# Wide cross-attention: value and output weights folded per head, context multiplied by them in dense chunks through DRAM, dense probabilities, one exponential per eight heads

## The chip, the cores and the metric

One Trainium2 chip, one core of it. The metric is the device time of one execution in microseconds (us), the median of several runs. The engines are TensorE (PE, with its weight loads as PEld), VectorE (DVE), ScalarE (ACT), GpSimd (POOL) and SyncE (SP); transfers issued by SyncE and ScalarE run as hardware queues.

## The reference

Two decoder layers over `x` of 64 sequences x 128 tokens x 128 channels. The kernel has six stages: Taylor attention, **wide cross-attention**, GELU experts, causal attention, rotary cross-attention, SwiGLU experts. The change touches the second (with residual and layer norm around it). Cut to what matters, for each sequence (SQ = 128 tokens, SK = 77 context tokens, 16 heads of 64):

```
xn   = layernorm(x) * gamma + beta                       # 128 x 128
q    = xn @ w_q                                          # 128 x 1024, 16 heads
k, v = split(context @ w_kv)                             # 77 x 1024 each, 16 heads
p    = softmax(q_h @ k_h.T * 64 ** -0.5, axis=-1)        # 128 x 77, each head
o    = concat_h(p_h @ v_h) @ w_out + b_out               # 128 x 128
x    = layernorm(x + tanh(gate) * o)
```

Then the router of the next stage takes logits of the new `x`, picks two of eight experts for each token, and the tokens are scattered to DRAM, sorted by expert.

## The kernel before

`softmax_attention(chip, "wide", ...)` works on pairs of sequences, 32 in all. Each engine has its own program, written out by hand; the engines meet in semaphores. A loop step has eight slots `k` (`NU` = 8; a slot is four heads of one of the pair's two sequences). In a step different pairs are at different stages: `f` is the pair whose front is made (layer norm, keys, values), `c` the pair whose scores are made (one step later), `u` the one before that, and `n`, `r`, `q`, `ranked` and `later` are older pairs in layer norm, router and scatter. `lagged(c, u, k, lag)` finds the piece of `lag` slots ago. The order of work within a slot is the order in the code, on each engine, and a waiting instruction holds up all behind it on its engine.

Query and key weights are already folded per head at the start of the stage (`product`, 128 x 128 for each head), so the keys of a head are `product` times the context. What one pair does now:

- TensorE: 16 key products of 154 columns in six groups (`front_pe`, m 0 to 5), four value products of 512 columns (m 6 to 9), the transpose of `xn` (m 10); eight score products of 308 columns (four heads x 77); 32 transposes of probabilities, 128 x 77 each (`TLAG` 3 slots later); 32 context products (`PLAG` 4 slots later), each with 64 columns of weights in half the array; at `Y_AT` 6 `project`, 16 products of 128 x 128 with `wo_scaled`. Each product of fp32 data is two instructions in the trace, a transpose one.
- VectorE: for each slot the negated maximum (`neg_max`), a reciprocal of the four sums; for every second slot the copy of the context products to `oT`; `add_and_measure` at `Z_AT` 7; both layer norms; the router's chains of small instructions (`place_block`).
- ScalarE: copies of keys, values and transposed probabilities out of PSUM, and 32 exponentials of 77 columns, one for each head, with the maximum as bias and the sum as accumulator.
- GpSimd: for each slot `probs` = `exps` x `inv_sum`; parts of the layer norms, the residual, and the indirect scatters.
- SyncE: for pair f the load of `xin` (it waits for `z_done` of pair f-4: `RING` = 4 buffers) and of `ctxT`. After the loads of pairs 7, 15, 23 and 31 it issues a quarter of the fill of the second `sorted_x` with blanks, on the same queue; nothing waits for that fill before a much later stage.

Opening the stage, TensorE makes `product` and VectorE scales the output weights with tanh(gate) (`wo_scaled`).

Of the kernel before, what the change touches and what calls it, by code (L numbers as in the profile page):

```python
# [22 lines left out]
P = 128  # L23
F32 = mybir.dt.float32
# [369 lines left out]
def softmax_attention(chip, kind, n_seq, X, ctxT_dram, w, consts, route=None, fill=None, opening=None, later_loads=()):  # L394
# [13 lines left out]
    FU = {"wide": 11, "causal": 4, "rotary": 2}[kind]  # L408
# [14 lines left out]
    with ExitStack() as ctx:  # L423
# [10 lines left out]
        values = sb("values", [P, 2, 2, H, STRIP])  # L434
        keys = sb("keys", [P, 2, H, 2, NK] if kind == "wide" else [P, 2, KH, NK])
        exps = sb("exps", [P, ES, HU, NK])
        if late:
            sums = sb("sums", [P, 2, NC * P])
            inv_total = sb("inv_total", [P, 2, H])
            o = sb("o", [P, 2, H, 8])  # L440
        else:
            exp_sum = sb("exp_sum", [P, SLOTS, HU])
            inv_sum = sb("inv_sum", [P, SLOTS, HU])
            probs = sb("probs", [P, SLOTS, HU, NK])
        probsT = sb("probsT", [P, 2, HU * P])
        neg_max = sb("neg_max", [P, SLOTS, HU])
        oT = sb("oT", [P, 2, 2, P] if late else [P, 2, 2, NC, P])
# [6 lines left out]
        if kind != "causal":  # L454
            ctxT = sb("ctxT", [P, RING, 2, P])
        if kind == "wide":
            xn = sb("xn", [P, 2, P])
# [4 lines left out]
            product = sb("product", [P, H, P])  # L462
# [47 lines left out]
        f_bank, y_bank = chip.banks[:, 6], chip.banks[:, 7]  # L510
        free_at_first = [f_bank, y_bank] + s_bank + p_bank + o_bank
# [11 lines left out]
        READY = {"wide": 2, "causal": 5, "rotary": 5}[kind]  # L523
        ROOT = 3 + 3 * NEWTON
        PREPARED = {"wide": 3, "causal": 4, "rotary": 10}[kind]
# [40 lines left out]

        @block.sync
        def _(sp):
            def step(f):
                if f is None:  # L570
                    return
# [17 lines left out]
            run_steps(sp, step, n_pairs, 1, 4)  # L589
# [40 lines left out]
        def _(pool):  # L630
# [4 lines left out]
            if kind == "rotary":  # L635
                pool.memset(ctxT[:, :, :, NK:P], 0.0).then_inc(ready, 1)
            if kind != "wide":
# [27 lines left out]
            def step(e, roots, f, c, u, n, r=None, *later):  # L665
                for k in range(NU):
# [1442 lines left out]
```

## Time and profile before

| what | value |
|---|---|
| median of 3 runs | 2991.36 us (2991.24 to 2993.08) |
| span of the profiled execution | 3015.3 us |
| TensorE busy over the span | 2737.1 us, 91% |
| ScalarE, VectorE, GpSimd busy | 2070.9, 1805.1, 1460.1 us |
| mean granted clock of TensorE | 0.965 of full speed |
| the wide stage | from about 229 us to about 1145 us |

The span of the profiled execution is 0.8% longer than the median of the runs; nothing else is known of its own time. "Granted clock" is the share of the full TensorE clock of 2.4 GHz, so 0.50 is 1.2 GHz. In the wide stage the loop of 32 pairs runs to about 1098 us; behind it the last blocks of tokens are routed and scattered.

### The profile page before, as it was taken

The numbers are of one execution on the slowest core, as the hardware profiler recorded it, in microseconds if no ns is written. First come the engines' busy times: TensorE is split into PE (matmuls) and PEld (weight loads), VectorE is DVE, ScalarE is ACT, GpSimd is POOL, SyncE is SP. The second block draws the span as 40 slices with busy tenths as digits, with TensorE's granted clock in tenths as the row PEclk, the third lists the DMA queues.
The fourth block names the chain that finished last, engine by engine and source line by source line (L and its number), as shares of the span: only waits on it lengthen the run. The fifth ranks groups of instructions, "written<-read, shape, count | busy, mean of one in ns | idle before, by whom it ended". The sixth has DMA issues, their size and how long they took to land. (4 is left out here: it accounts for less than half of the span.)

```text
span 3015.3 us, 69304 instructions
## 1 busy us (share of the span) xinstructions
PE 2737.1 (91%) x21504; PEld 1982.6 (66%) x21504; DVE 1805.1 (60%) x5293; ACT 2070.9 (69%) x7235; POOL 1460.1 (48%) x1978
## 2 busy tenths in 40 slices
PE   8999999999999956998799999978999999699987
PEld 6666777777777746998355555546776666458874
DVE  6883344443444444554688888876677776444545
ACT  6766778777787743443699999976888888522224
POOL 3442224444444454555433333325678887724665
PEclk9999999999999987999899999998999999799998
DMA  9910030220400402221310000000000010001225
GB/s 264 338 47 15 19 116 16 80 78 20 129 27 20 135 30 72 73 70 57 115 56 10 9 10 8 10 22 10 13 27 28 29 31 17 29 26 56 80 79 185
DMA packets 179960, 185.08 MB, mean 61 GB/s; under 512 B 32844, under 2 KB 168537, under 8 KB 179216
## 3 DMA queue, kind: packets, MB, share of 16 engines
q1 hardware_dynamic: 162032, 145.14, 16.1%
q0 software_dynamic: 17280, 34.13, 3.4%
q8 instruction: 181, 2.97, 0.4%
q14 instruction: 179, 1.47, 0.2%
q10 hardware_dynamic: 288, 1.38, 0.2%
HBM read 58.34 MB, written 111.48 MB: 56 GB/s over the span
## 5 line engine op out<-in xcount | busy, mean ns | idle before, releaser
L678 POOL TENSOR_TENSOR wide_probs<-wide_exps,wide_inv_sum 128x308 f32<-128x308 f32 x256 | 179.3, 700 | 488.9 <-DVE wide_inv_sum L1409 486.0
L1400 DVE TENSOR_REDUCE wide_neg_max<-banks 128x4 f32<-128x308 f32 x256 | 122.5, 478 | 473.6 <-PE banks L982 448.9
L1116 ACT ACTIVATE causal_exps<-causal_biased,causal_neg_max 128x128 f32<-128x128 f32 x1024 | 325.8, 391 | 31.1 <-DVE causal_neg_max L1400 29.7
L1119 ACT ACTIVATE wide_exps<-banks,wide_neg_max 128x77 f32<-128x77 f32 x1024 | 315.8, 326 | 0.3 <-DVE wide_neg_max L1400 0.2
L658 POOL DMA_INDIRECT sorted_x<-send,place_i x240 | 244.9, 1020 | 96.0 <-issue 40.5
L1116 ACT ACTIVATE rotary_exps<-banks,rotary_neg_max 128x77 f32<-128x77 f32 x1024 | 252.0, 351 | 15.1 <-DVE rotary_neg_max L1400 13.7
L1103 ACT ACTIVATE wide_probsT<-banks 77x512 f32<-77x512 f32 x256 | 152.1, 594 | 153.6 <-PE banks L991 149.5
L1656 ACT ACTIVATE gelu_hidden<-banks,gelu_slot 128x256 f32<-128x256 f32 x284 | 116.7, 471 | 157.3 <-PE banks L1833 153.1
L1587 POOL DMA_INDIRECT results<-swiglu_tile_out,swiglu_dest_i x142 | 147.7, 1040 | 141.2 <-DVE swiglu_tile_out L1738 97.8
L1119 ACT ACTIVATION_READ_ACCUMULATOR wide_exps<-banks,wide_neg_max 128x1 f32 x1024 | 213.9, 209 | 0.0
L1587 POOL DMA_INDIRECT results<-gelu_tile_out,gelu_dest_i x142 | 140.8, 991 | 142.3 <-DVE gelu_tile_out L1743 119.0
L1358 DVE TENSOR_TENSOR causal_biased<-banks,regions 128x512 f32<-128x512 f32 x256 | 164.6, 685 | 72.3 <-PE banks L968 69.9
L1400 DVE TENSOR_REDUCE rotary_neg_max<-banks 128x4 f32<-128x308 f32 x256 | 121.5, 475 | 120.8 <-PE banks L982 116.4
L982 PE MATMUL banks<-wide_keys,wide_xT 128*128 128x308 f32 x512 | 191.8, 455 | 1.9 <-ACT wide_xT L769 1.6
L982 PE MATMUL banks<-rotary_keys,rotary_qT 128*128 128x308 f32 x512 | 189.0, 451 | 3.5 <-ACT rotary_exps L1116 3.4
L616 POOL TENSOR_TENSOR rotary_keys<-rotary_kT,rest 128x308 f32<-128x308 f32 x256 | 177.4, 708 | 20.0 <-ACT rotary_kT L803 16.5
L991 PEld LDWEIGHTS banks<-first,causal_exps 128*128 128x128 f32 x1024 | 108.9, 141 | 116.3 <-ACT causal_exps L1116 61.0
L1103 ACT ACTIVATE rotary_probsT<-banks 77x512 f32<-77x512 f32 x256 | 157.7, 616 | 34.7 <-PE banks L991 34.1
L735 PE MATMUL banks<-wide_ctxT,wide_product 128*128 128x154 f32 x1024 | 169.9, 299 | 3.3 <-ACT wide_product L1038 0.7
L1400 DVE TENSOR_REDUCE causal_neg_max<-causal_biased 128x4 f32<-128x512 f32 x256 | 169.6, 673 | 0.5 <-ACT causal_exps L1116 0.4
L991 PE MATMUL banks<-first,causal_exps 128*128 128x128 f32 x1024 | 166.1, 285 | 3.1 <-ACT causal_exps L1116 3.0
L1014 PE MATMUL banks<-wide_probsT,wide_values 77*64 77x128 f32 x2048 | 168.3, 285 | 0.1
(382 smaller groups left out, 7339.3 us busy)
## 6 DMA issues: line engine op xcount, KB each, us to landing
sorted_x<-blank SPq DMA_DIRECT2D x1, 34848.0 KB, 116.8
sorted_x<-blank SPq DMA_DIRECT2D x4, 8712.0 KB, 30.3
gelu_tile_in<-sorted_x SPq DMA_DIRECT2D x71, 132.0 KB
swiglu_tile_in<-sorted_x SPq DMA_DIRECT2D x71, 132.0 KB
gelu_back<-results SPq DMA_DIRECT2D x16, 512.0 KB, 7.7
swiglu_back<-results SPq DMA_DIRECT2D x16, 512.0 KB, 6.2
X<-in_x SPq DMA_DIRECT2D x8, 512.0 KB, 7.3
regions<-in_g_w SPq DMA_DIRECT2D x2, 2048.0 KB, 20.9
```

The source lines that it names most:

```text
L616: engine.tensor_tensor(keys[:, b, heads], kT[:, pair.c % 2, b, 0:NK].unsqueeze(1).to_broadcast([P, HU, NK]), mask[:, heads].unsqueeze(2).t ...
L658: pool.indirect_dma_start(route["sorted_x"], bass.IndirectOffsetOnAxis(ap=r_place_i[:, b % 2, which, n // 2:n // 2 + 1], axis=0), send[:, ...
L678: pool.tensor_tensor(probs[:, m % SLOTS], exps[:, m % SLOTS], inv_sum[:, m % SLOTS].unsqueeze(2).to_broadcast([P, HU, NK]), ALU.mult).then ...
L735: last = pe.matmul(f_bank[:, n * 2 * NK:(n + 1) * 2 * NK], product[:, first + n], ctxT[:, s4, :, 0:NK], start=True, stop=True)
L982: pe.matmul(s_bank[k % 2][:, 0:HU * NK], q, moving, start=True, stop=True).then_inc(s_ps, 1)
L991: last = pe.transpose(p_bank[n % 2][0:NK, h * P:(h + 1) * P], exps[:, (NU * pair.c + n) % ES, h] if late else probs[:, n % SLOTS, h], ident)
L1014: last = pe.matmul(o_bank[g % 2][row:row + STRIP, col:col + P], values[0:NK, pair.c % 2, b, first_head(j) + h], probsT[0:NK, n % 2, h * P: ...
L1103: act.activation(probsT[0:NK, n % 2], p_bank[n % 2][0:NK], ACT.Copy).then_inc(probsT_done, 1)
L1116: last = act.activation(exps[:, (NU * c.c + k) % ES, h], scores[:, h * NK:(h + 1) * NK], ACT.Exp, bias=neg_max[:, k % SLOTS, h:h + 1])
L1119: last = act.activation(exps[:, k % SLOTS, h], scores[:, h * NK:(h + 1) * NK], ACT.Exp, bias=neg_max[:, k % SLOTS, h:h + 1], accum_out=exp ...
L1400: dve.tensor_reduce(neg_max[:, k % SLOTS], scores.rearrange("p (h n) -> p h n", h=HU), AX.X, ALU.max, negate=True).then_inc(max_done, 1)
L1587: pool.indirect_dma_start(results, bass.IndirectOffsetOnAxis(ap=dest_i[:, t % YR, j:j + 1], axis=0), tile_out[:, t % YR, j], None, bounds_ ...
```

## The change

It computes the same with other intermediate values.

- At the start of the stage the value weights and the output weights of each head are multiplied (`fold`, 128 x 2048: 16 heads of 128 x 128, scaled with tanh(gate)). `wo_scaled` and `project` are gone, and so are `values`, `oT` and `o_done` for this stage.
- The context of all sequences is read as 4928 tokens in a row, in 39 chunks of 128 (the last of 64). A chunk times `fold` is four units of 512 columns (`unit`), 156 in all. Three are made ahead of the loop, then five a step, at the slots `V_AT`. ScalarE copies each from `o_bank[1]` to `staged` (`keep_unit`).
- SyncE stores each chunk (1 MB) to `v_dram` and loads it back for each pair in eight transfers (`load_folded`), so that a row of `folded` is one (context token, head), in chunks of 128 rows, five for eight heads (616 rows). The issues for pair t-2 stand behind the loads for pair t in SyncE's program, and behind the fill where there is one.
- The scores have their maximum subtracted by VectorE, into `exps`; one exponential on ScalarE then covers eight heads (616 columns, in place); VectorE sums it, takes the reciprocal, and GpSimd writes the product in the order (token, head).
- The probabilities are transposed in five chunks of 128 for eight heads (`turn_probs`, `TLAG` 4), and `weighted_sum` (`PLAG` 5) adds all 20 products of a pair's two sequences in `o_bank[0]`, which VectorE adds to the residual (`Z_AT` 5). `weighted_sum` of a pair waits for its eight loads and for the last pair's `z`.
- Each pair's `ctxT` for the keys stays; the chunks of context are loaded once more (`v_context`). The wait of `turn_tokens` for `z_done` is dropped in this stage.

```diff
-    FU = {"wide": 11, "causal": 4, "rotary": 2}[kind]
+    FU = {"wide": 7, "causal": 4, "rotary": 2}[kind]
+    HH, PARTS, CHUNKS, SPARE, VU, V_EARLY, EB = 8, 8, 5, 2, 5, 3, 3
+    TOKENS = n_seq * CONTEXT
+    N_UNITS = 4 * ((TOKENS + P - 1) // P)
...
+            def store_chunk(n):
+                rows = min(P, TOKENS - P * n)
+                sp.wait_ge(v_done, 4 * n + 4)
+                sp.dma_start(route["v_dram"][:, P * n:P * n + rows].rearrange("g t c -> t g c"),
+                             staged[0:rows, n % 2].rearrange("p (g c) -> p g c", g=2)).then_inc(v_stored[n % 2], 16)
+
+            def load_folded(pair):
+                last = (2 * CONTEXT * (pair + 1) - 1) // P
+                for n in range(max(0, last - 1), last + 1):
+                    sp.wait_ge(v_stored[n % 2], 16 * (n // 2 + 1))
+                if pair >= SPARE:
+                    sp.wait_ge(pv_done, PARTS * (pair - SPARE + 1))
+                for b in range(2):
+                    for g in range(2):
+                        t = CONTEXT * (2 * pair + b)
+                        sp.dma_start(folded[:, pair % SPARE, b, g, 0:4],
+                                     route["v_dram"][g, t:t + 64].rearrange("(c k) (h d) -> (k h) c d", c=4, h=HH)).then_inc(folded_loaded[pair % SPARE], 16)
+                        sp.dma_start(folded[0:104, pair % SPARE, b, g, 4],
+                                     route["v_dram"][g, t + 64:t + CONTEXT].rearrange("k (h d) -> (k h) d", h=HH)).then_inc(folded_loaded[pair % SPARE], 16)
+
+            def values_step(pair):
+                if pair == 0:
+                    sp.wait_ge(ready, READY)
+                made = (V_EARLY + VU * pair) // 4
+                for n in range(made if pair else 0, min((V_EARLY + VU * (pair + 1)) // 4, N_UNITS // 4)):
+                    store_chunk(n)
+                load_folded(pair)
+
...
+            def step(f, ahead=None, pair=None):
+                if f is not None:
+                    load(f)
+                if kind == "wide" and pair is not None:
+                    values_step(pair.c)
+
+            def load(f):
+                if kind == "wide":
...
-            run_steps(sp, step, n_pairs, 1, 4)
+            run_steps(sp, step, n_pairs, 3 if kind == "wide" else 1, 4)
...
-                    at = None if late else lagged(c, u, k, MLAG)
+                    at = None if late or k % 2 else lagged(c, u, k, 2)
                     if at is not None:
-                        pair, m = at
-                        pool.wait_ge(inv_done, pair.count(NU, m + 1))
-                        if before(pair, m, SLOTS) is not None:
-                            bc, bk = before(pair, m, SLOTS)
-                            pool.wait_ge(probsT_ps, bc.count(NU, bk + 1))
-                        pool.tensor_tensor(probs[:, m % SLOTS], exps[:, m % SLOTS],
-                                           inv_sum[:, m % SLOTS].unsqueeze(2).to_broadcast([P, HU, NK]), ALU.mult).then_inc(probs_done, 1)
+                        half = 4 * at[0].c + at[1] // 2
+                        pool.wait_ge(inv_done, half + 1)
+                        if half >= SLOTS:
+                            pool.wait_ge(probsT_ps, 2 * (half - SLOTS) + 2)
+                        pool.tensor_tensor(probs[:, half % SLOTS, 0:HH * NK].rearrange("p (k h) -> p h k", h=HH), exps[:, half % EB],
+                                           inv_sum[:, half % SLOTS].unsqueeze(2).to_broadcast([P, HH, NK]), ALU.mult).then_inc(probs_done, 1)
...
+        V_AT = [0, 2, 4, 6, 7]
+        FRONT_AT = {"wide": [(0, 0), (1, 0), (2, 0), (3, 0), (4, 0), (5, 0), (7, 0)],
                     "causal": [(0, 0), (1, 0), (2, 0), (3, 0)], "rotary": [(5, 0), (7, 0)]}[kind]
...
-        TLAG, PLAG, OLAG = (2, 3, 4) if late else (3, 4, 5)
-        Y_AT, Z_AT = 6, 7
+        TLAG, PLAG, OLAG = (2, 3, 4) if late else (4, 5, 6)
+        Z_AT = 5
...
+            def unit(v):
+                rows = chunk_rows(v)
+                if v >= 1:
+                    pe.wait_ge(v_done, v)
+                if v % 4 == 0:
+                    pe.wait_ge(v_context_loaded[v // 4 % 4], 16 * (v // 16 + 1))
+                pe.matmul(v_bank[0:rows], v_context[:, v // 4 % 4, 0:rows], fold[:, (v % 4) * 512:(v % 4 + 1) * 512],
+                          start=True, stop=True).then_inc(v_ps, 1)
...
+                for n in range(H // 2):
+                    last = pe.transpose(p_bank[n // 4][:, (n % 4) * P:(n % 4 + 1) * P], w["wv"][:, n * P:(n + 1) * P], ident)
+                    if n % 4 == 3:
+                        last.then_inc(wvT_ps, 1)
+                pe.wait_ge(wvT_done, 2)
+                for n in range(H // 2):
+                    for odd in range(2):
+                        rows = slice(64 * odd, 64 * odd + 64)
+                        last = pe.matmul((p_bank if odd else o_bank)[n // 4][:, (n % 4) * P:(n % 4 + 1) * P], wvT[rows, n], w["wo"][rows, n],
+                                         start=True, stop=True)
+                    if n % 4 == 3:
+                        last.then_inc(fold_ps, 1)
                 pe.wait_ge(product_done, UB)
+                pe.wait_ge(fold_done, 4)
                 pe.wait_ge(prepared, PREPARED)
+                for v in range(V_EARLY):
+                    unit(v)
...
-            def project(u, r, q):
-
-                pe.wait_ge(o_done, u.count(OG, OG))
-                if u.back(1).real:
-                    pe.wait_ge(z_done, u.back(1).count(1, 1))
-                if r is not None:
-                    pe.wait_ge(logits_done, r.count(1, 1))
-                if block_of(q, 3) is not None:
-                    pe.wait_ge(base_done, block_of(q, 3) + 1)
-                for b in range(2):
-                    for n in range(NC):
-                        last = pe.matmul(y_bank[:, b * P:(b + 1) * P], oT[:, u.c % 2, b, n],
-                                         w["wo_scaled" if kind == "wide" else "wo"][:, n], start=n == 0, stop=n == NC - 1)
-                last.then_inc(y_ps, 1)
+            def turn_probs(pair, m):
+                half, part = 4 * pair.c + m // 2, m % 2
+                if part == 0:
+                    pe.wait_ge(probs_done, half + 1)
+                if half >= 1:
+                    pe.wait_ge(probsT_done, 2 * half + part - 1)
+                for n in range(2 if part else 3):
+                    at = (3 * part + n) * P
+                    last = pe.transpose(p_bank[part][:, n * P:(n + 1) * P], probs[:, half % SLOTS, at:at + P], ident)
+                last.then_inc(probsT_ps, 1)
+
+            def weighted_sum(pair, m):
+                half, part = 4 * pair.c + m // 2, m % 2
+                b, g = m // 4, m // 2 % 2
+                pe.wait_ge(probsT_done, 2 * half + part + 1)
+                if m == 0:
+                    pe.wait_ge(folded_loaded[pair.c % SPARE], 16 * 8 * (pair.c // SPARE + 1))
+                    if pair.c >= 1:
+                        pe.wait_ge(z_done, pair.c)
+                for n in range(3 * part, CHUNKS if part else 3):
+                    last = pe.matmul(o_bank[0][:, b * P:(b + 1) * P], probsT[:, half % 2, n * P:(n + 1) * P], folded[:, pair.c % SPARE, b, g, n],
+                                     start=g == 0 and n == 0, stop=g == 1 and n == CHUNKS - 1)
+                last.then_inc(pv_done, 1)
...
+            def keep_unit(v):
+                rows, n = chunk_rows(v), v // 4
+                act.wait_ge(v_ps, v + 1)
+                if v % 4 == 0 and n >= 2:
+                    act.wait_ge(v_stored[n % 2], 16 * (n // 2))
+                act.activation(staged[0:rows, n % 2, (v % 4) * 512:(v % 4 + 1) * 512], v_bank[0:rows], ACT.Copy).then_inc(v_done, 1)
...
+                        half, part = 4 * at[0].c + at[1] // 2, at[1] % 2
+                        columns = slice(3 * P, CHUNKS * P) if part else slice(0, 3 * P)
+                        act.wait_ge(probsT_ps, 2 * half + part + 1)
+                        if half >= 2:
+                            act.wait_ge(pv_done, 2 * half + part - 3)
+                        act.activation(probsT[:, half % 2, columns], p_bank[part][:, 0:(2 if part else 3) * P], ACT.Copy).then_inc(probsT_done, 1)
...
+                    if c is not None and not late and k % 2 == 1:
+                        half = 4 * c.c + k // 2
+                        act.wait_ge(shifted_done, 2 * half + 2)
+                        act.activation(exps[:, half % EB], exps[:, half % EB], ACT.Exp).then_inc(exps_done, 1)
...
+                for n in range(2):
+                    dve.wait_ge(wvT_ps, n + 1)
+                    dve.tensor_copy(wvT[:, 4 * n:4 * n + 4].rearrange("p n c -> p (n c)"), p_bank[n]).then_inc(wvT_done, 1)
+                dve.wait_ge(prepared_ps, UB)
+                by_parity = fold.rearrange("p (n odd d) -> p n odd d", odd=2, d=P)
+                for n in range(2):
+                    dve.wait_ge(fold_ps, n + 1)
+                    for odd in range(2):
+                        dve.tensor_scalar(by_parity[:, 4 * n:4 * n + 4, odd], (p_bank if odd else o_bank)[n].rearrange("p (n d) -> p n d", d=P),
+                                          w["tanh_gate"], None, ALU.mult).then_inc(fold_done, 1)
...
+                    at = None if late or k % 2 else lagged(c, u, k, 2)
+                    if at is not None:
+                        half = 4 * at[0].c + at[1] // 2
+                        dve.wait_ge(exps_done, half + 1)
+                        dve.tensor_reduce(exp_sum[:, half % SLOTS], exps[:, half % EB], AX.X, ALU.add).then_inc(sum_done, 1)
+                        if half >= SLOTS:
+                            dve.wait_ge(probs_done, half - SLOTS + 1)
+                        dve.wait_ge(sum_done, half + 1)
+                        dve.reciprocal(inv_sum[:, half % SLOTS], exp_sum[:, half % SLOTS]).then_inc(inv_done, 1)
...
+                        if kind == "wide":
+                            half = 4 * c.c + k // 2
+                            if half >= EB:
+                                dve.wait_ge(probs_done, half - EB + 1)
+                            dve.wait_ge(max_done, c.count(NU, k + 1))
+                            dve.tensor_tensor(exps[:, half % EB, HU * (k % 2):HU * (k % 2 + 1)], scores.rearrange("p (h n) -> p h n", h=HU),
+                                              neg_max[:, k % SLOTS].unsqueeze(2).to_broadcast([P, HU, NK]), ALU.add).then_inc(shifted_done, 1)
...
+            "fold": cut(region_b, 0, [P, 16 * P]), "product": cut(region_b, 16 * P, [P, 16, P]),
```

## Rows read from the trace of the kernel before

**Rows 1.** The page's first line, and busy us of each engine in one stretch of 100 us
```profile
span 3015.3 us, 69304 instructions
...
500.00:600.00 100.00, 99.06 (x733) 74.62 (x731) 44.24 (x163) 77.16 (x328) 44.68 (x64) 1.00 0.18 55
```

**Rows 2.** SyncE's timeline: start us, duration us, issue; loads of pairs 4 and 31
```profile
293.18 0.46 SPq L576 DMA_DIRECT2D wide_xin<-X  x1
...
1015.44 0.47 SPq L576 DMA_DIRECT2D wide_xin<-X  x1
```

**Rows 3.** TensorE's timeline in one pair: start us, duration us, group
```profile
607.30 1.08 PE L739 MATMUL banks<-regions,wide_ctxT 128*77 128x512 f32 x2
608.22 3.73 PE L944 MATMUL banks<-regions,wide_oT 128*128 128x128 f32 x32
611.79 0.69 PE L982 MATMUL banks<-wide_keys,wide_xT 128*128 128x308 f32 x2
...
617.60 0.68 PE L982 MATMUL banks<-wide_keys,wide_xT 128*128 128x308 f32 x2
618.13 0.60 PE L991 MATMUL banks<-first,wide_probs 128*77 128x128 f32 x4
618.56 0.95 PE L735 MATMUL banks<-wide_ctxT,wide_product 128*128 128x154 f32 x6
619.44 0.66 PE L1014 MATMUL banks<-wide_probsT,wide_values 77*64 77x128 f32 x8
620.03 0.61 PE L886 MATMUL banks<-rest,wide_tokensT 128*128 128x8 f32 x4
```

**Rows 4.** ScalarE's groups of the whole span: busy us, mean ns, idle before
```profile
L1116 ACT ACTIVATE causal_exps<-causal_biased,causal_neg_max 128x128 f32<-128x128 f32 x1024 | 325.8, 391 | 31.1 <-DVE causal_neg_max L1400 29.7
L1119 ACT ACTIVATE wide_exps<-banks,wide_neg_max 128x77 f32<-128x77 f32 x1024 | 315.8, 326 | 0.3 <-DVE wide_neg_max L1400 0.2
...
L774 ACT ACTIVATE wide_keys<-banks 128x462 f32<-128x462 f32 x160 | 89.1, 557 | 26.3 <-PE banks L735 25.4
```

**Rows 5.** VectorE's groups, of the page and of the stretch 400 to 1000 us
```profile
L1400 DVE TENSOR_REDUCE wide_neg_max<-banks 128x4 f32<-128x308 f32 x256 | 122.5, 478 | 473.6 <-PE banks L982 448.9
...
L1358 DVE TENSOR_TENSOR causal_biased<-banks,regions 128x512 f32<-128x512 f32 x256 | 164.6, 685 | 72.3 <-PE banks L968 69.9
...
L1400 DVE TENSOR_REDUCE causal_neg_max<-causal_biased 128x4 f32<-128x512 f32 x256 | 169.6, 673 | 0.5 <-ACT causal_exps L1116 0.4
...
L1422 DVE COPY wide_oT<-banks 128x512 f32<-128x512 f32 x90 | 59.8, 664 | 0.3 <-issue 0.3
...
L1343 DVE TENSOR_TENSOR wide_z<-banks,wide_residual 128x256 f32<-128x256 f32 x22 | 8.7, 395 | 0.0
```

**Rows 6.** GpSimd's costliest group of the page
```profile
L678 POOL TENSOR_TENSOR wide_probs<-wide_exps,wide_inv_sum 128x308 f32<-128x308 f32 x256 | 179.3, 700 | 488.9 <-DVE wide_inv_sum L1409 486.0
```

**Rows 7.** DMA issues: count, KB each, median us from issue to landing
```profile
sorted_x<-blank SPq DMA_DIRECT2D x4, 8712.0 KB, 30.3
...
causal_xin<-X SPq DMA_DIRECT2D x32, 128.0 KB, 2.0
...
regions<-in_alibi ACTq DMA_DIRECT2D x1, 1024.0 KB, 5.1
...
regions<-in_rest SPq DMA_DIRECT2D x1, 16.0 KB, 17.0
```

**Rows 8.** Stretches: engines as in rows 1, then granted clock, DMA share, GB/s
```profile
10.00:15.00 5.00, 4.75 (x24) 3.58 (x23) 1.14 (x3) 2.02 (x8) 0.79 (x2) 1.00 1.20 290
...
230.00:235.00 5.00, 5.00 (x25) 5.00 (x25) 2.14 (x11) 1.71 (x3) 1.44 (x3) 0.50 0.65 169
...
240.00:241.00 1.00, 1.00 (x10) 1.00 (x9) 0.00 (x0) 0.60 (x2) 0.00 (x0) 1.00 0.00 0
...
380.00:400.00 20.00, 19.81 (x143) 14.07 (x142) 7.52 (x25) 14.35 (x61) 4.90 (x7) 1.00 1.09 340
...
1104.00:1106.00 2.00, 0.00 (x0) 0.00 (x0) 0.79 (x4) 0.66 (x3) 1.39 (x3) 0.50 0.10 34
```

More of the change, by code:

```diff
@@ L433, in softmax_attention @@
         xT = sb("xT", [P, 2, 2, P])
-        values = sb("values", [P, 2, 2, H, STRIP])
+        if kind != "wide":
+            values = sb("values", [P, 2, 2, H, STRIP])
         keys = sb("keys", [P, 2, H, 2, NK] if kind == "wide" else [P, 2, KH, NK])
-        exps = sb("exps", [P, ES, HU, NK])
+        exps = sb("exps", [P, ES, HU, NK] if late else [P, EB, HH, NK])
         if late:
@@ L461, in softmax_attention @@
             pre_rstd = sb("pre_rstd", [P, 2])
-            product = sb("product", [P, H, P])
+            product = w["product"]
         else:
@@ L636, in _ @@
                 pool.memset(ctxT[:, :, :, NK:P], 0.0).then_inc(ready, 1)
+            if kind == "wide":
+                pool.memset(probs[:], 0.0).then_inc(ready, 1)
+                pool.memset(folded[:, :, :, :, CHUNKS - 1], 0.0).then_inc(ready, 1)
             if kind != "wide":
@@ L730, in front_pe @@
             if kind == "wide":
-                if m <= 5:
-                    first = 3 * m
-                    wait_loaded(pe, f)
-                    for n in range(min(3, H - first)):
-                        last = pe.matmul(f_bank[:, n * 2 * NK:(n + 1) * 2 * NK], product[:, first + n], ctxT[:, s4, :, 0:NK],
-                                         start=True, stop=True)
-                else:
-                    b, half = divmod(m - 6, 2)
-                    last = pe.matmul(f_bank[0:NK, :], ctxT[:, s4, b, 0:NK], w["wv"][:, half * 512:(half + 1) * 512],
-                                     start=True, stop=True)
+                first = 3 * m
+                wait_loaded(pe, f)
+                for n in range(min(3, H - first)):
+                    last = pe.matmul(f_bank[:, n * 2 * NK:(n + 1) * 2 * NK], product[:, first + n],
+                                     ctxT[:, s4], start=True, stop=True)
                 return last
@@ L1000, in step @@
                     at = lagged(c, u, k, PLAG)
-                    if at is not None:
+                    if at is not None and not late:
+                        weighted_sum(*at)
+                    if at is not None and late:
                         pair, n = at
@@ L1018, in step @@
                         front(f, k, 1)
+                    if kind == "wide" and units_at(f, c, k) is not None:
+                        unit(units_at(f, c, k))
                     if late:
@@ L1049, in front @@
                                 act.wait_ge(s_ps, f.back(2).count(NU, NU))
-                            if m == (6 if kind == "wide" else 3):
+                            if late and m == 3:
                                 act.wait_ge(pv_done, f.back(2).count(NU, NU))
@@ L1373, in step @@
                         add_and_measure(n)
+                    if not late and u is not None and k == Z_AT:
+                        add_and_measure(u)
                     for turn, pair in enumerate((r, q) + later[1:3]):
@@ L1460, in step @@
                         divide(u, (k - 4) // 2)
-                    if u is not None and not late and k == Z_AT:
-                        add_and_measure(u)
             run(dve, step, STAGES)
```

152 lines of the change are left out of this document (84 added, 68 removed).

## The prediction

> **What bounds the kernel now.** I read the page first, then the busy time of each engine in stretches of 100 us, to find where the changed stage lies and which engine is full in it. In such a stretch TensorE is busy 99.06 of 100 us at a granted clock of 1.00, with ScalarE at 77.16, VectorE at 44.24 and GpSimd at 44.68 [rows 1]. The reader should see that only TensorE has nothing left. SyncE's timeline gives the pace: the load of `xin` for pair f waits for `z` of pair f-4, so the distance between two loads is one pair. Between the two rows shown lie 27 pairs in 722.26 us, 26.75 us each [rows 2]. The stage has 32 such pairs. Last, TensorE's own timeline: its groups start back to back, and the distance from one start to the next is what a group really costs (the durations printed overlap, and are longer).
>
> By those starts a score group costs 0.53 us, four transposes of probabilities 0.43, six key products 0.88, a value product of 512 columns (two instructions) 0.92, a group of eight context products 0.59, and the 32 instructions of the output projection 3.57, 0.112 each [rows 3].
>
> **TensorE.** Scores, keys, `xn`, tokens and the router stay, so only the difference counts, per pair [rows 3]:
> - Transposes: 32 (8 groups, 3.4 us) become 20, since the 616 columns of eight heads fill five chunks of 128. 20 x 0.43/4 = 2.2 us: -1.3.
> - Values: 4 products of 512 columns (3.7 us) become 156 units over 32 pairs, 4.9 a pair, 4.5 us: +0.8. The folded value is twice as wide (16 heads x 128), though tokens are packed into full chunks.
> - Context and projection: 8 x 0.59 + 3.57 = 8.3 us become 20 products of two instructions. I take the projection's 0.112 for each of the 40, as it has the same shape and accumulates too: 4.5 us, -3.8. The bound below is a context instruction's 0.074, another -1.5.
>
> Together -4.3 us: TensorE alone would allow 22.4 us a pair, and 32 pairs give -138 us.
>
> **ScalarE.** 32 exponentials of 77 columns (326 ns, each with a read of its accumulator) go; four of 616 columns come. A copy of 462 columns took 557 ns, in proportion 0.74 us for 616; exponentials of 128 and 77 columns took 391 and 326, and that slope drawn out gives 1.0. I take 0.8, nearer to the long copy: 3.2 us in all [rows 4]. ScalarE falls from 0.77 x 26.75 = 20.6 to some 15 us. It bounds nothing; it matters as a wait for VectorE. Its new `keep_unit` also waits for the store of two chunks before; behind it stand the exponentials, but that store has had over a step to land.
>
> **VectorE.** 0.442 x 26.75 = 11.8 us now [rows 1]. Four copies of 512 columns (664 ns) go, and the saving on reciprocals I leave out. New are eight subtractions of the maximum on 308 columns: the nearest rows are 395 ns for 256 and 685 for 512, so 0.46, and the bound above is the whole 685. Four sums over 616 columns: maxima over 308 and 512 took 478 and 673 ns, so 0.77. Sum: 11.8 - 2.7 + 3.7 + 3.1 = 15.9 us [rows 5]. But VectorE now waits before each sum for the exponential that its own subtraction has just released: one exponential and two handovers, 1.0 us, more if ScalarE is at a key copy (0.56). Four waits make 19.9 us on average. The router's small dependent instructions fall on two of each four pairs, and those then need some 23.5 us, over TensorE's 22.4. I add 0.5 us a pair: 22.9, which gives back 16 us in all. Two score banks lie between that ring and TensorE, so smaller delays don't reach it.
>
> **GpSimd.** Eight multiplications of 308 columns (700 ns) become four of 616: between 0.7 and 1.4 us in proportion, and writing with a stride of eight might double the last. Its result is wanted some 8 us after the scores, and exponential, sum, reciprocal and multiplication need about 5. Hidden, up to 2.8 us as well [rows 6].
>
> **The start of the stage.** Ahead of the first front there are now eight transposes, two copies, 32 instructions of folding, four scalings and three units. TensorE works there at the clock 0.50 until 240 [rows 8], so what costs 0.11 costs 0.22: transposes 1.8, copy 0.7, fold 5 (the clock rises on the way), last scalings 1.4, units with their copies 5, less 3 for units that the loop is spared: 11 us. Pair 0 also wants its folded values in a short first step, 2 us: +13. The stage's end (routing and scatter of the last block) stays.
>
> **The trip through DRAM.** Per pair SyncE now stores 1.2 chunks of 1 MB and loads 1.26 MB back in eight transfers with pieces of 512 bytes. In normal pairs this is hidden under the scores of the next step. In the worst phase of four pairs a chunk is complete 1 us into that step; the store lands after 5.1 us (so did the load of the slopes, 1 MB), eight issues at 0.6 take 5, the landing 2: 13 us, and the weighted sum wants it at about 17 us [rows 7].
>
> That cover is gone four times. On the same queue SyncE fills `sorted_x` with 8712 KB after its loads for pairs 7, 15, 23 and 31, and this takes 30.3 us [rows 7]. Today nothing is late, since `xin` is loaded far ahead. In the change the fill goes out ahead of the folded values of the pair two behind. Follow pair 5, in steps of the loop of 22.9 us and eight slots. The load for pair 7 waits for `z` of pair 3, which VectorE adds in slot 5 of step 5: 5.64. The weighted sum of pair 5 begins in slot 5 of step 6, behind that slot's scores, transposes and keys: 6.70. That is 24 us. If the queue's transfers run in order, they need 1.6 (issues before the fill) + 30.3 + 3.5 for the store of chunk 7 (1 MB at some 300 GB/s; the stretches have 290 and 340 [rows 8]) + 7.4 (eight issues and a landing, as SyncE awaits that store) = 43 us. TensorE stands 18.5 us. At the three later fills the loads want older stores and queue directly: 1.6 + 30.3 + 3.5 + 4.3 (1.26 MB at the 290 of the load of X, also in 512-byte pieces) = 40, and TensorE stands 15.5. Four fills: 65 us. That transfers run in order is what a small one shows: 16 KB issued behind 4 MB of expert weights landed after 17.0 us, where 128 KB on an idle queue took 2.0 [rows 7]. With fair sharing the loads would be at most some 2 us late.
>
> The Trainium skill, "DMA: Bandwidth & Descriptors", section "Queues, rings and completion order", says that each DMA engine consumes the descriptors of a ring in ring order, and that all of SyncE's transfers use one row of rings. The landing after 17.0 us agrees. By that rule the four waits come and the sum is 2965 us; without it it is 2887.
>
> After each wait TensorE is cold: two us after its last matmul of a stretch the granted clock was 0.50, and after the barrier before this stage it came back only at 240, 11 us after work had begun [rows 8]. Eleven us at half rate lose 5.5 us, the bound above; below it is nothing. I take 4, near the measured case, as the waits are shorter: 16 us.
>
> **The sum.** -138 + 16 + 13 + 65 + 16 = -28 us on the profiled span of 3015.3 us [rows 1], -0.93%. The profiled execution is 0.8% longer than the median of 2991.36, so the share is what I carry over: 2964, said as 2965 us.
>
> **Rivals.**
> - *No collision* (the transfers of a queue share the engines). Against it stands the landing after 17.0 us; for it only that a transfer with an older one of 8 MB ahead is seen nowhere. Then -138 + 16 + 13 + 4 = -105: 2887 us. Chance 0.2.
> - *The ring of VectorE and ScalarE sets the pace* (the slower side). For it: VectorE needs 19.9 of 22.4 us by my values, and with 0.685 for a subtraction and waits of 1.4 it is 23.3 and more with the router. Against it: the interpolated rows. At 25 us a pair the loop gains 56 us and the rest costs 94: +38, 3029 us. It decides from 26.75 - 94/32 = 23.8 us a pair on. Chance 0.22.
> - *The folded values are late in other pairs too*, as the margin is 4 us and the pieces are small. At 2 us a pair, 64 more: 3029 us. Chance 0.08.
>
> The forecast, four collisions and a loop near 22.9, has 0.5, and its own range is 2935 to 2990 us. The range for 8 in 10 reaches from the first rival, 2880, to near the slower ones, 3020. About 0.2% is what a measurement here tells from no change. Faster: 0.2 + 0.48 = 0.68; same: 0.05; slower: 0.27.
>
> **What would show it.** The distance between `xin` loads is 22 to 23.5 us, and at four places near 40. TensorE's idle time is put down to the DMA of the folded values at these four and hardly elsewhere, with the clock at 0.50 behind each. In the loop VectorE is near 70% busy, ScalarE's exponential takes 0.7 to 1.0 us, GpSimd's product 0.7 to 2.8, and a weighted sum's instruction 0.112. I am wrong if the four gaps are missing, or if in each pair TensorE waits for the subtraction, or for `wide_probs`.

## The result, and the profile after

2890.3 us median (2889.8 to 2891.3) against 2992.2 us before, ratio 0.966 (95% interval 0.965 to 0.968): 102 us faster. The forecast was 2965 us, 26 us faster. The range of 2880 to 3020 holds the result, but the gain is nearly four times the one forecast. It landed beside the figure of the rival "no collision", 2887 us, and for another reason than that rival's: the collisions are all there.

One number must be read with care. The profiled execution of before is 24 us longer than its median, and the excess lies in the last stage: 372.1 us there (2643.2 to 3015.3 us) against 344.5 us in the profile after. The change does not touch that stage. The wide stage itself takes 916.2 us before (229.0 to 1145.2) and 820.1 after (226.9 to 1047.0), 96 us less; that is the difference to explain.

The page after: its first line, the engines, and TensorE's 40 slices of 72 us. The wide stage is slices 4 to 15. Four dips among them, slices 6, 8, 11 and 13 (digits 7, 7, 7 and 8), are where TensorE stands; slices 14 and 15 (6 and 3) hold the end of the fourth stop and the stage's end:

```profile
span 2888.3 us, 63045 instructions
...
PE 2554.6 (88%) x19424; PEld 1891.0 (65%) x19424; DVE 1952.0 (68%) x5426; ACT 1830.7 (63%) x5343; POOL 1441.1 (50%) x1852
...
PE   8998979799798639997899999968999999779996
```

SyncE's timeline after, the same issue as in [rows 2], around the first fill, and then a stretch without one:

```profile
353.46 0.47 SPq L654 DMA_DIRECT2D wide_xin<-X  x1
...
354.61 0.46 SPq L664 DMA_DIRECT2D sorted_x<-blank  x1
357.92 19.74 SPq L607 DMA_DIRECT2D v_dram<-wide_staged  x1
386.19 0.36 SPq L619 DMA_DIRECT2D wide_folded<-v_dram  x1
...
390.28 0.47 SPq L654 DMA_DIRECT2D wide_xin<-X  x1
...
414.85 0.47 SPq L654 DMA_DIRECT2D wide_xin<-X  x1
435.15 0.47 SPq L654 DMA_DIRECT2D wide_xin<-X  x1
...
517.49 0.47 SPq L654 DMA_DIRECT2D wide_xin<-X  x1
```

The reader should see two things. From 435.15 to 517.49 lie four pairs: 20.6 us each, where 22.9 were forecast. And the two distances at the fill, 36.8 and 24.6 us, are 20 us more than two such pairs. The store behind the fill takes 19.74 us to issue, and the first folded load goes only at 386.19, 31.6 us after the fill.

TensorE's waits from 240 to 1010 us (engine, line, who released it: us in total, times, longest), and its timeline at the first fill:

```profile
PE banks L1050 <- issue: 71.7, 4, 18.6
PE banks L1050 <- DVE wide_z L1484: 3.4, 2, 2.3
PE banks L895 <- ACT wide_staged L1155: 3.1, 7, 0.7
PE banks L1088 <- DVE wide_exps L1559: 2.9, 4, 1.0
PE banks L1050 <- DMA wide_folded<-v_dram: 2.4, 1, 2.4
```

```profile
374.23 0.43 PE L814 MATMUL banks<-wide_ctxT,regions 128*128 128x154 f32 x2
393.31 1.62 PE L1050 MATMUL banks<-wide_folded,wide_probsT 128*128 128x128 f32 x6 [18.65 <-issue]
```

L1050 is `weighted_sum`. It stands 71.7 us in four waits, and hardly anything else holds TensorE up. The profile puts them down to "issue" and names no transfer; that it is the folded values is shown by the runs below. The first instructions behind the wait last 1.62 us for six, against 0.83 elsewhere.

Now a slot of TensorE after and the beginnings of two more, to be laid beside [rows 3]:

```profile
462.42 0.69 PE L1088 MATMUL banks<-wide_keys,wide_xT 128*128 128x308 f32 x2
462.95 0.49 PE L1038 MATMUL banks<-first,wide_probs 128*128 128x128 f32 x3
463.27 0.95 PE L814 MATMUL banks<-wide_ctxT,regions 128*128 128x154 f32 x6
464.06 0.61 PE L1050 MATMUL banks<-wide_folded,wide_probsT 128*128 128x128 f32 x4
...
470.57 1.02 PE L895 MATMUL banks<-regions,wide_v_context 128*128 128x512 f32 x2
471.43 0.69 PE L1088 MATMUL banks<-wide_keys,wide_xT 128*128 128x308 f32 x2
```

By starts: three transposes 0.32 us, as forecast. But the group of six key instructions (three products; the prediction calls them six), which the change does not touch, takes 0.79 us where it took 0.88, and a unit of 512 columns 0.86 where a value product took 0.92. The groups that "stay" got cheaper.

### The profile page after: what moved, and what is told of

Same layout as the page of the kernel before. It is cut to its first block and busy times, and to the rows that moved or that the text cites. A ratio compares the mean times of both kernels' runs of the same rounds, so it can differ in the third digit from the quotient of the medians.

```text
span 2888.3 us, 63045 instructions
## 1 busy us (share of the span) xinstructions
PE 2554.6 (88%) x19424; PEld 1891.0 (65%) x19424; DVE 1952.0 (68%) x5426; ACT 1830.7 (63%) x5343; POOL 1441.1 (50%) x1852
## 3 DMA queue, kind: packets, MB, share of 16 engines
q14 instruction: 164, 1.34, 0.2%
## 5 line engine op out<-in xcount | busy, mean ns | idle before, releaser
L758 POOL TENSOR_TENSOR wide_probs<-wide_exps,wide_inv_sum 128x616 f32<-128x616 f32 x128 | 168.3, 1315 | 385.8 <-DVE wide_inv_sum L1538 299.9
L1050 PE MATMUL banks<-wide_folded,wide_probsT 128*128 128x128 f32 x1280 | 191.1, 281 | 78.1 <-issue 71.7
L1050 PEld LDWEIGHTS banks<-wide_folded,wide_probsT 128*128 128x128 f32 x1280 | 172.0, 197 | 80.4 <-issue 77.6
L1225 ACT ACTIVATE wide_probsT<-banks 128x384 f32<-128x384 f32 (+1 forms) x256 | 111.4, 435 | 132.2 <-PE banks L1038 116.0
L694 POOL TENSOR_TENSOR rotary_keys<-rotary_kT,rest 128x308 f32<-128x308 f32 x256 | 177.3, 708 | 20.0 <-ACT rotary_kT L874 16.6
L1088 PE MATMUL banks<-wide_keys,wide_xT 128*128 128x308 f32 x512 | 183.3, 439 | 2.9 <-DVE wide_exps L1559 2.9
L777 POOL TENSOR_TENSOR causal_var_eps<-causal_mean_var,causal_eps 128x2 f32<-128x2 f32 x32 | 6.3, 196 | 328.1 <-DVE causal_mean_var L1491 328.1
L895 PE MATMUL banks<-regions,wide_v_context 128*128 128x512 f32 (+1 forms) x312 | 164.5, 609 | 4.9 <-ACT wide_staged L1155 3.1
```

The source lines that it names most:

```text
L694: engine.tensor_tensor(keys[:, b, heads], kT[:, pair.c % 2, b, 0:NK].unsqueeze(1).to_broadcast([P, HU, NK]), mask[:, heads].unsqueeze(2).t ...
L758: pool.tensor_tensor(probs[:, half % SLOTS, 0:HH * NK].rearrange("p (k h) -> p h k", h=HH), exps[:, half % EB], inv_sum[:, half % SLOTS].u ...
L895: pe.matmul(v_bank[0:rows], v_context[:, v // 4 % 4, 0:rows], fold[:, (v % 4) * 512:(v % 4 + 1) * 512], start=True, stop=True).then_inc(v_ ...
L1050: last = pe.matmul(o_bank[0][:, b * P:(b + 1) * P], probsT[:, half % 2, n * P:(n + 1) * P], folded[:, pair.c % SPARE, b, g, n], start=g == ...
L1088: pe.matmul(s_bank[k % 2][:, 0:HU * NK], q, moving, start=True, stop=True).then_inc(s_ps, 1)
```

## The experiments

The kernel after, unless another base is named, and times beside the kernel before on the same chip (2990 to 2992 us).

**1. The fill in pieces behind the loads.** `FILLS` is 33 here, and the block in `load(f)` is gone.

```diff
                 if kind == "wide" and pair is not None:
                     values_step(pair.c)
+                    for m in ((31, 32) if pair.c == 31 else (pair.c,)):
+                        rows, cleared, blank = fill
+                        n = SORTED_ROWS // P // 2 // FILLS
+                        sp.dma_start(rows.rearrange("(p j k) d -> p j (k d)", p=P, k=2)[:, n * m:n * (m + 1)],
+                                     blank.unsqueeze(1).to_broadcast([P, n, 2 * ROW])).then_inc(cleared, 16)
```

> The fill is cut into 33 pieces of 1056 KB, one issued behind the folded loads of each pair (two behind the last). Theory O (the loop stands four times because the folded values queue behind a fill of 8712 KB): the four waits of 16.6 to 18.7 us and the cold clock behind them go, about 20 us each, 80 in all: 2810 us (2800 to 2825). Rival S (the DMA engines are simply too full in those stretches, whatever the order): a piece of 3.7 us in each pair makes all pairs a little late, the total stays near 2890 us. Rival V (without the waits the ring of VectorE and ScalarE takes over): the waits go but the pairs get longer, 2840 to 2870 us.

Measured: 2812.7 us (2810.4 to 2813.3), ratio to before 0.940 (0.939 to 0.942). The four waits are gone, and the pairs stay at 20.1 to 21.6 us, as between the fills of the kernel after. Theory O holds, S and V fall: the same bytes in the same stage cost next to nothing (2.2 us more than in experiment 4, where they are elsewhere) when no transfer stands long in front.

**2. The same fills from another queue.** The block moves from SyncE's `load(f)` to ScalarE's program, `act.dma_start(...)` at slot 6 of the step two earlier.

> The same four fills of 8712 KB, issued by ScalarE (its own queue) in slot 6 of the step of the pair for which SyncE is about to store and load. Theory O (order within SyncE's queue): the store and the loads now share the DMA engines with the fill instead of standing behind it, take about twice their time (store 7, loads 9 us) and just reach the weighted sum: waits of 0 to 5 us each, 2820 to 2835 us. Rival S (what counts is that the engines are full, not the queue): waits stay at 15 us or more each, 2880 to 2895 us.

Measured: 2840.1 us. TensorE's waits in the stage, as above:

```profile
PE banks L1044 <- issue: 21.9, 4, 9.2
```

21.9 us in four waits, the longest 9.2, where O expected at most 5 each and S at least 15. Order in one queue is most of the wait. The rest, more than I had allowed, comes with the fill in flight on another queue: it goes when the fill is cut up (experiment 1) or leaves the stage (experiment 4). Shared DMA engines would explain it; no run separates them from anything else.

**3. The same fills on the same queue, behind the folded loads of the step.** Only the place in SyncE's `step` differs: the block comes after `values_step`.

> The same four fills on SyncE's queue, but issued behind the folded loads of that step instead of ahead of them; they then stand ahead of the store and the loads of the next pair, whose weighted sum lies about 1.5 steps on instead of one. Theory O: the fill is issued near step 6.2, ends near 7.7, the chunk's store and the loads land near 8.2, the weighted sum wants them at 7.7: waits of 8 to 12 us each instead of 18, 2855 us (2840 to 2870). Rival S: no difference from 2890.

Measured: 2861.4 us. The four waits are 11.8, 12.2, 9.1 and 9.3 us, and the last of them is put down to the transfer by name:

```profile
937.49 1.62 PE L1050 MATMUL banks<-wide_folded,wide_probsT 128*128 128x128 f32 x6 [9.33 <-DMA wide_folded<-v_dram]
```

So the waits are the folded values, and their length follows from when the next loads are wanted: counted in steps as in the prediction, 8 to 12 us were expected, and the longest came to 12.2.

**4. The fills in the causal stage.** The argument `fill` is taken from the call for "wide" and given to the call for "causal".

> The four fills are issued in the causal stage, at the same four places of that stage's loop, and none in the wide stage. Theory O: wide stage without the four waits, the causal stage unchanged (its xin is loaded four pairs ahead): 2810 us, the same as with the pieces or up to 5 us less. If the pairs of the wide stage are 20.4 us throughout, the loop is bound by TensorE alone; if they lengthen with the waits gone, another ring is near.

Measured: 2810.5 us (2808.7 to 2811.8), ratio to before 0.940 (0.938 to 0.941), the fastest version, level with the pieces. Against the kernel after that is 79.8 us, 20.0 for each fill: 17.9 of wait, and 2 left over for the cold clock. In a stretch of 100 us of its loop, which answers to [rows 1]:

```profile
460.00:560.00 100.00, 99.95 (x626) 80.26 (x625) 77.58 (x223) 66.03 (x145) 57.03 (x65) 1.00 0.47 145
```

TensorE is full, and VectorE has gone from 44 to 78.

**5. What a change of weight width costs.** Base: experiment 4. One tiny product, read by nobody, ahead of each score product; `cols` is 64 in the one run and 128 in the other.

```diff
                             if kind == "wide":
+                                pe.matmul(s_bank[k % 2][0:cols, 400:408], ident[:, 0:cols], ident[:, 0:8], start=True, stop=True)
                                 q = xT[:, c.c % 2, b]
```

> Base is the kernel with the fills in the causal stage (2810.5 us). Ahead of each of the 256 score products one tiny product of 8 columns is added, with 64 columns of weights (half the array), whose result nobody reads. Theory M (the kernel before paid near 0.1 us each time TensorE went between full-width weights and the half-width ones of its context products, and the change is faster than the forecast because it has none): the slot grows by the two small instructions, 0.15 to 0.18 us, plus two switches, 0.2: about 0.36 us, 90 us in all, 2900 us. Rival N (no price for a switch; the groups were dearer before for other reasons, such as the 77 columns or the waits between them): no more than the full-width twin, 45 us or less, 2855 us.

> The twin of the half-width run: the same tiny product of 8 columns, with all 128 columns of weights. The router's four small instructions of 8 columns take 0.36 us, so 0.18 us a slot, 46 us in all: 2856 us under both theories. Under M the half-width run is some 45 us slower than this one, under N equal or a little faster, as its weight load is shorter.

Measured: 2897.5 us with 64 columns, 2858.6 with 128. The half-width product is the smaller one and costs 38.9 us more over 256 slots, 0.15 us a slot (by the distances between pairs in the loop, 23.5 against 22.2 us, it is 0.17). Where it goes, half width first, then full width:

```profile
475.25 1.02 PE L895 MATMUL banks<-regions,wide_v_context 128*128 128x512 f32 x2
476.20 0.28 PE L1083 MATMUL banks<-first 128*64 128x8 f32 x2
476.42 0.79 PE L1089 MATMUL banks<-wide_keys,wide_xT 128*128 128x308 f32 x2
```

```profile
474.24 1.02 PE L895 MATMUL banks<-regions,wide_v_context 128*128 128x512 f32 x2
475.10 0.28 PE L1083 MATMUL banks<-first 128*128 128x8 f32 x2
475.24 0.77 PE L1089 MATMUL banks<-wide_keys,wide_xT 128*128 128x308 f32 x2
```

The unit in front lasts 0.95 against 0.86 us by starts, and the tiny product itself 0.22 against 0.14. Going to 64 columns costs about 0.09 us and going back about 0.08. The printed durations of the unit and of the tiny product are the same in both runs, so the switch is seen in the starts alone. Theory M, size included.

The kernel after has a change of width of its own: the last chunk has 64 tokens, so its four units have 64 columns of weights. Such a unit takes 1.01 us by starts where a full one takes 0.86:

```profile
922.35 1.07 PE L895 MATMUL banks<-regions,wide_v_context 128*64 128x512 f32 x2
923.36 0.79 PE L1088 MATMUL banks<-wide_keys,wide_xT 128*128 128x308 f32 x2
923.99 0.38 PE L1038 MATMUL banks<-first,wide_probs 128*128 128x128 f32 x2
```

The score group behind it takes 0.63 us, against 0.53 behind a full unit.

**6. The kernel before without half-width products.** Base: the kernel before. Each context product gets 128 columns of weights, `values[0:NK, ..., at_head:at_head + 2]`, and writes all 128 rows of its bank, so that heads overwrite each other.

> The kernel before, with each context product given 128 columns of weights (two heads' values) in place of 64 in half the array; the upper and lower halves overwrite each other, so the context of half the heads is wrong in this run and only its time counts. Two half-width products no longer run side by side, so a group of eight costs 8 x 0.107 = 0.86 us instead of 0.59: +0.27 us a slot, 69 us over 256 slots. Theory M: the key or value group ahead loses 0.1 us and the group behind up to 0.1: net +0.08 us a slot, 3010 us (3000 to 3020). Rival N: the full 69 us, 3059 us.

Measured: 3004.2 us, ratio to before 1.005 (1.003 to 1.006), +13 us where N expected +69 and M +20. Its timeline:

```profile
624.26 0.95 PE L735 MATMUL banks<-wide_ctxT,wide_product 128*128 128x154 f32 x6
625.05 1.05 PE L1016 MATMUL banks<-wide_probsT,wide_values 77*128 77x128 f32 x8
625.94 0.51 PE L886 MATMUL banks<-rest,wide_tokensT 128*128 128x8 f32 x4
```

A context group now takes 0.89 us in place of 0.59, and the key group ahead of it is down to 0.79 from 0.88, exactly what it takes after the change. The transposes of 77 columns are still there: 77 against 128 columns costs nothing, only half width does. Going by time, 77 us of longer groups (0.30 x 256) came out as 13, so the switches of the kernel before are worth up to 64 us. That is an upper bound. Three of a pair's eight context groups, between two key or two value groups, took 0.72 or 0.76 us before and not 0.59. The value products behind two of them waited for ScalarE's copy of the values, which is no switch. These three make 15 of the 64 us; the other 49 lie in the groups around the context groups.

**7. VectorE loaded.** Base: experiment 4, with a second `tensor_reduce` of each half into a spare buffer.

> Base with the fills in the causal stage. VectorE sums each 616-column half twice (once into a buffer that nobody reads): +0.8 us four times a pair, 3.2 us. Theory R (the ring VectorE - ScalarE stands close behind TensorE: 16.1 us of work and four waits of 0.65 to 1.0 in a pair of 20.4): pairs grow by 1.5 to 3 us, 50 to 95 us in all, 2860 to 2905 us. Rival T (VectorE's idle 22% is real slack): under 10 us, 2815 us.

Measured: 2886.1 us, +76. Pairs last 23.1 us (four from 427.49 to 519.72), 2.5 more for 3.2 us of added work. VectorE, with what it waits for, stands right behind TensorE; the longest of TensorE's waits is now that of `weighted_sum` for `z`, about half of the 54 us by which this stretch's 22 pairs grew (TensorE's waits from 400 to 900 us):

```profile
PE banks L1051 <- DVE wide_z L1485: 26.8, 18, 1.9
```

**8. Two exponentials of four heads in place of one of eight.** Base: experiment 4.

```diff
-                    if c is not None and not late and k % 2 == 1:
-                        half = 4 * c.c + k // 2
-                        act.wait_ge(shifted_done, 2 * half + 2)
-                        act.activation(exps[:, half % EB], exps[:, half % EB], ACT.Exp).then_inc(exps_done, 1)
+                    if c is not None and not late:
+                        half, part = 4 * c.c + k // 2, slice(HU * (k % 2), HU * (k % 2 + 1))
+                        act.wait_ge(shifted_done, 2 * half + k % 2 + 1)
+                        last = act.activation(exps[:, half % EB, part], exps[:, half % EB, part], ACT.Exp)
+                        if k % 2 == 1:
+                            last.then_inc(exps_done, 1)
```

> Base with the fills in the causal stage (2810.5 us). The exponential over eight heads is split again into two of four heads (308 columns), each as soon as its own subtraction is done; VectorE's sum still waits for both. ScalarE works some 0.2 us more four times a pair, but the last exponential in front of the sum takes 0.45 instead of 0.72 us, so the ring with VectorE gets shorter. If TensorE alone sets the pace (theory T): no change beyond 3 us either way, and then one exponential over eight heads is worth nothing over two of four. If the ring costs something now (theory R, as the doubled sum lengthened the pairs at once): 2 to 10 us faster, 2800 to 2808 us. If ScalarE's own order gets in the way (rival): 5 to 15 us slower.

Measured: 2813.1 us (2812.3 to 2814.5), 2.6 us more than experiment 4. The two ran on different chips, and the kernel before took 1.3 us more on this one (2991.5 against 2990.3). Theory T: TensorE sets the pace, the ring costs nothing as long as it is shorter. Covering eight heads rather than four with one exponential is worth nothing that can be told.

## Why the prediction was wrong

Its sum, term by term, against the wide stage's -96 us:

| term | forecast | measured |
|---|---|---|
| TensorE's work per pair, x 32 | -138 | -197 (26.75 to 20.6 us) |
| ring of VectorE and ScalarE | +16 | 0 (any delay by it is in the pair's 20.6) |
| start of the stage | +13 | +14 (first score product 18.3 us after the stage's start before, 32.6 after) |
| four collisions | +65 | +72 |
| cold clock behind them | +16 | +8 |
| sum | -28 | -103 |

The measured column goes 7 us beyond the stage's own difference; 32 times a mean over four pairs is no finer than that.

- **The step that failed** is "Scores, keys, `xn`, tokens and the router stay, so only the difference counts". Their work stays, but their price depended on their neighbours. Between the key products at full width and the context products at half width, TensorE changed over twice a slot. The 0.88 us of a key group held 0.09 of that, the 0.92 of a value product 0.06, and the group behind held the rest. The change puts every product of the loop at full width but the four units of the last chunk. Experiment 5 gives 39 us for this over 256 slots, experiment 6 up to 64; the term was 59 us short. The rows to see it were on record: behind a context group the same score group costs 0.63 us, behind the projection or a value product 0.53. In the kernel before:

```profile
604.63 0.69 PE L982 MATMUL banks<-wide_keys,wide_xT 128*128 128x308 f32 x2
605.16 0.60 PE L991 MATMUL banks<-first,wide_probs 128*77 128x128 f32 x4
...
623.01 0.79 PE L982 MATMUL banks<-wide_keys,wide_xT 128*128 128x308 f32 x2
623.64 0.60 PE L991 MATMUL banks<-first,wide_probs 128*77 128x128 f32 x4
```

How the 59 divides can be read from TensorE's timelines, with the start-to-start distances summed over 16 pairs of the loop (before from 345.95 us, experiment 6 from 347.29, experiment 4 from 393.48), in us a pair:

| groups | before | experiment 6 | experiment 4 |
|---|---|---|---|
| keys, scores, tokens, transposes of `xn` and `X` ("stay") | 10.66 | 9.42 | 9.32 |
| context products and projection, then weighted sums | 8.74 | 10.70 | 4.57 |
| values, then units | 3.74 | 3.46 | 4.35 |
| transposes of probabilities | 3.47 | 3.47 | 2.17 |

The groups that stay are 1.34 us a pair cheaper, 43 us of the 59. Experiment 6 takes 1.24 of it without the change, by full-width context products alone, so it is the width and not the rest of the rewriting. Most of what is left is the context groups: they cost 0.65 us on average, and the forecast took the 0.59 of one of them, so they were 14 us more to lose. How much of these 14 is width and how much the wait for ScalarE's copies is open.

The Trainium skill, "TensorEngine Tiling (Array Packing)", section "Key Properties", says that changing the tiling mode drains TensorE. Experiments 5 and 6 agree in that a change of width costs time, 0.15 us there and back; what TensorE does in that time no trace shows. By that rule the forecast should have credited up to 8 x 0.15 to 0.25 us a pair, 39 to 64 us.

- **Transposes, units, weighted sums** by themselves were priced right: 0.108, 0.86 and 0.112 us (0.67 for six) against 0.108, 0.92 and 0.112.
- **The ring**: VectorE's work was priced right, the ring's hold on TensorE was not. VectorE's work came to 78.9% of 20.6 us, 16.3 us (15.9 forecast); ScalarE's exponential took 0.72 us, GpSimd's product 1.32. VectorE stood 0.62 us ahead of each sum where 1.0 was forecast (43.7 us in 70 times), so the ring had 18.8 of 20.6 us and not 19.9 of 22.4. The 0.5 us a pair that I added for the router's pairs did not come; that the two score banks took it in is likely, but no run shows it. Experiment 7 shows how near it was.
- **The collisions** came where they were forecast, and nearly as long: 18.65, 17.9, 18.6 and 16.6 us, against 18.5 and three of 15.5. The match of the first is luck. From the load of `xin` to the end of the wait 39.9 us passed (353.46 to 393.31), not 43, but with faster pairs the weighted sum wanted the values after 21.2 us, not 24. At the third the 40 us were right (39.7), but the values were wanted 3 us earlier than forecast, and the wait grew by that. They begin in `weighted_sum` in slot 5 of the next step. Their cause is the order in SyncE's queue for two thirds (experiment 2 takes 50 of 72 us away); the rest needs the fill in flight at the same time. The small transfer that landed after 17.0 us [rows 7] had told it.
- **The cold clock** costs 2 us for each, not 4: the four groups behind the first wait take 3.9 us (393.31 to 397.21), and the same groups take 2.0 elsewhere. TensorE had stood still for 18.65 us. Engines and granted clock (as in [rows 8]) behind that wait:

```profile
394.00:396.00 2.00, 2.00 (x9) 1.54 (x8) 0.01 (x1) 0.00 (x0) 0.00 (x0) 0.50 0.79 322
396.00:398.00 2.00, 2.00 (x9) 1.59 (x8) 0.95 (x2) 0.49 (x1) 0.00 (x0) 0.71 0.12 33
398.00:400.00 2.00, 2.00 (x14) 1.63 (x13) 0.96 (x2) 1.55 (x4) 0.00 (x0) 1.00 0.85 253
```

The clock is back about 4 us after work began, against 11 us at the stage's start [rows 8].
- **The rivals.** "No collision" is refuted though its time was met: the 59 us of the changes of width and the 16 of the ring are together about what the collisions and the cold clock cost (80), and only the trace tells them apart. "The ring sets the pace" would come true with some 0.7 us more of VectorE's work in a pair, an estimate from experiment 7 (3.2 added, 2.5 came through). Late values in other pairs were not seen: one wait of 2.4 us at pair 0, as forecast.

## What to carry to other kernels

When a change rewrites part of an engine's stream, price the groups that stay as well: read their start-to-start distances by what stands before and behind them, and look for changes of width in the weights. Before adding a round trip to a queue, list what else is on that queue and how long it takes; a transfer that nobody waits for is not harmless once something urgent stands behind it, and cutting it into pieces or moving it to a stage with far prefetch removed nearly all of an 80 us cost (2812.7 and 2810.5 us). An engine at 78% can be the next bound when it waits four times a pair for what another engine makes of its own product.

## What the runs showed of the hardware that was not expected

- A change of TensorE between 128 and 64 columns of weights costs 0.09 us on the way there and 0.08 back (experiment 5), and isn't in the printed durations of the groups on either side of the change there. Between 128 and 77 columns it costs nothing that the starts show: a key group between them takes 0.79 us in experiment 6, as between groups of 128.
- VectorE's normalisation of `xn` (128 x 128, from SBUF) took 706 ns after the change against 359 before, with the same shape:

```profile
L1585 DVE TENSOR_SCALAR wide_xn<-wide_xin,wide_pre_mean_var,wide_pre_rstd 128x128 f32<-128x128 f32 x36 | 21.7, 706 | 0.0
```

GpSimd's product is 1315 ns long in place of 700, and is still running when it starts (470.14 for 1.33 us, and 470.92). VectorE's same operation on `X` in the same stage took 358 ns. That the two engines block each other there was not tested.
- Issuing a store took 19.74 us where 0.4 is usual, when 8.7 MB stood in front on the same queue, and 21.4 to 22.0 us behind the three later fills: an engine that issues transfers is held up itself.
